# A gated cross-attention and expert block: the routing tiles' copies on ScalarE, their residual on TensorE, a head more on VectorE

## The reference

```python
xn   = layernorm(x)                                   # 4096 tokens x 256
kv   = ctx @ W_kv.T + b_kv                            # per token: 16 keys, 16 values of 16 numbers
s    = einsum('bshd,bstd->bsht', q, k) / 4            # 16 heads attend to 16 heads of the SAME token
co   = einsum('bsht,bstd->bshd', softmax(s), v)
x    = x + tanh(g_xattn) * (co @ W_out.T + b_out)
xn   = layernorm(x)
p    = softmax(xn @ gate_w.T)                         # 8 experts; each takes its 64 best of 256 tokens
h    = gelu(xn[chosen] @ w1[e]) @ w2[e]               # 256 -> 1024 -> 256
x    = x + tanh(g_ffn) * scatter_add(p[chosen] * h)
```

## Time and profile before

| | |
|---|---|
| time, median of 3 runs | 699.21 us (699.01 to 699.41) |
| profiled execution, its own time | 700.73 us |
| span of its trace | 698.7 us |
| mean granted PE clock | 0.976 of full speed |
| busy: PE, DVE, ACT, POOL | 660.8, 597.7, 433.0, 535.4 us |

### The profile page before, as it was taken

One profiled execution on the slowest core, in us unless ns is written; L12 is line 12 of the kernel. 1 busy time (PEld: TensorE's weight loads), 2 busy tenths in 40 slices (PEclk: granted clock), 3 DMA queues, 4 the chain that ended last, 5 costly groups with the idle time before them and its releaser, 6 DMA issues.

```text
span 698.7 us, 11584 instructions
## 1 busy us (share of the span) xinstructions
PE 660.8 (95%) x3921; PEld 539.8 (77%) x3921; DVE 597.7 (86%) x786; ACT 433.0 (62%) x1081; POOL 535.4 (77%) x498
## 2 busy tenths in 40 slices
PE   8999989978799999989999999989999999999996
PEld 5566566534688888878888888868888899999995
DVE  6999999899999999998999999999999251586763
ACT  5677677655777777766777778747766533232321
POOL 4899899897878888988888889888898516435343
PEclk8999999989999999999999999989999999999999
DMA  3876798461558787776788877767777858999993
GB/s 126 304 260 207 229 306 261 177 242 49 190 181 247 241 268 237 221 229 187 222 245 250 242 242 226 234 173 240 227 233 223 269 177 281 327 311 303 322 269 38
DMA packets 97073, 160.96 MB, mean 230 GB/s; under 512 B 8171, under 2 KB 74486, under 8 KB 97014
## 3 DMA queue, kind: packets, MB, share of 16 engines
q1 hardware_dynamic: 84006, 142.78, 61.1%
q0 software_dynamic: 12288, 16.79, 12.9%
q10 hardware_dynamic: 720, 0.66, 0.3%
HBM read 126.63 MB, written 33.55 MB: 229 GB/s over the span
## 4 chain that ended last, share of the span: by engine, by line
PE 67%; DMA 10%; issue 7%; POOL 6%; DVE 6%; ACT 3%; POOLq 0%; DVEq 0%; ACTq 0%
PE bank L1176 21%; PE bank L1159 19%; DMA out_dram<-ys,ids 8%; PE bank L1086 6%; PE bank L1203 4%; PE bank L1106 4%; PE bank L1039 3%; PE bank L1193 3%; DVE prod_v L492 2%; POOL prod_p L344 2%; PE bank L1145 2%; DVE co L494 1%; PE bank L1118 1%; DMA xg<-xn_scratch,ids 1%; POOL tree_a L352 1%
## 5 line engine op out<-in xcount | busy, mean ns | idle before, releaser
L1159 PE MATMUL bank<-xin,w1in 128*128 128x256 f32 x1536 | 205.0, 291 | 5.3 <-issue 4.9
L1159 PEld LDWEIGHTS bank<-xin,w1in 128*128 128x128 f32 x1536 | 193.8, 196 | 6.8 <-issue 6.1
L1176 PE MATMUL bank<-w2s,hT 128*128 128x256 f32 x768 | 175.4, 382 | 0.0
L415 POOL DMA_INDIRECT out_dram<-ys,ids x64 | 105.0, 1640 | 76.8 <-ACT ys L865 57.7
L1176 PEld LDWEIGHTS bank<-w2s,hT 128*128 128x128 f32 x768 | 142.4, 190 | 17.7
L851 ACT ACTIVATE hT<-bank 128x512 f32<-128x512 f32 x128 | 76.0, 597 | 107.7 <-PE bank L1159 107.1
L494 DVE TENSOR_REDUCE co<-prod_v 128x208 f32<-128x3328 f32 (+2 forms) x32 | 109.7, 3428 | 1.1
L492 DVE TENSOR_TENSOR prod_v<-bank,Ex 128x3328 f32<-128x3328 f32 (+2 forms) x32 | 109.6, 3424 | 0.1
L352 POOL TENSOR_TENSOR tree_a<-prod_p 128x512 f32<-128x512 f32 (+2 forms) x64 | 85.8, 1341 | 4.7
L401 POOL DMA_INDIRECT xg<-xn_scratch,ids x64 | 63.9, 998 | 31.8 <-issue 17.0
L344 POOL TENSOR_TENSOR prod_p<-kvs,q 128x1024 f32<-128x1024 f32 (+2 forms) x28 | 80.1, 2859 | 8.1 <-ACT q L819 6.4
(11 more groups left out here) (157 smaller groups left out, 1150.4 us busy)
## 6 DMA issues: line engine op xcount, KB each, us to landing
w1in<-w_parts SPq DMA_DIRECT2D x128, 512.0 KB, 5.3
w2s<-in_L_ffn_w_dram SPq DMA_DIRECT2D x32, 1024.0 KB, 5.7
w_parts<-w1s SPq DMA_DIRECT2D x32, 512.0 KB, 3.3
w1raw<-in_L_ffn_w_dram SPq DMA_DIRECT2D x32, 256.0 KB, 4.4
out_dram<-x SPq DMA_DIRECT2D x32, 128.0 KB, 4.2
xn_scratch<-xn SPq DMA_DIRECT2D x32, 128.0 KB, 2.5
xt<-in_x_dram SPq DMA_DIRECT2D x31, 128.0 KB, 5.2
ct<-in_ctx_dram SPq DMA_DIRECT2D x28, 128.0 KB, 4.7
```

The lines of the kernel that those rows point to most:

```text
L415: pool.indirect_dma_start(out=out_rows[:, :], out_offset=bass.IndirectOffsetOnAxis(ap=ids[:, g % 2, p * E + e:p * E + e + 1], axis=0), in_ ...
L1159: ins = pe.matmul(HB[k % 2][:, D * f:D * (f + 1)], w1in[:, k, w, c, P * f:P * (f + 1)].bitcast(f32r), xin[:, n % 2, x_, c, :], start=(m == ...
L1176: ins = pe.matmul(dst, hT[:, n % 2, f, cols], w2s[:, n % 2, f, :], start=(f == 0), stop=(f == FC - 1))
```

## The change

For the three tiles before a routing tile (9, 17, 25) `with_x` now holds: PE adds x by the identity product, ACT copies x2 out of PSUM, and DVE's `residual` in tiles 10, 18 and 26 is gone. `take_probs` and the gates of `routes` move from DVE to ACT, as `take_probs` and `take_gates` there, for all four groups. In a routing tile DVE takes 13 heads of the values and POOL three, where it was 12 and four. In the tile behind each (11, 19, 27) DVE takes 13 heads of the scores and POOL three, again for 12 and four. No DMA is added or dropped.

```diff
--- before.py
+++ after.py
@@ -26,7 +26,8 @@
     DC = D // P
     FC = F // P
     PR = BG // 2
-    START, EARLY, LATE, FIRST_ROUTING, ROUTING = (11, 11), (12, 11), (12, 13), (4, 12), (4, 12)
+    NEXT = (13, 13)
+    START, EARLY, LATE, FIRST_ROUTING, ROUTING = (11, 11), (12, 11), (12, 13), (4, 13), (4, 13)
     HR = 8
     HV, HP = max(LATE), H - min(ROUTING)
     EPS = 1e-5
@@ -41,16 +42,16 @@
     R2 = J * R0
     n1 = NT - N0 + 1
     gl = G - 1
-    routing = lambda s: s % TG == 2 and s > TG
     summed = lambda t: 0 < t < N0 - 1
     AHEAD = (14, 16, 23, 30)
     NA = len(AHEAD)
     plain = [u for u in range(NT) if u not in AHEAD]
     order = {u: j for j, u in enumerate(plain)}
-    with_x = lambda t: t < N0 - 2
-    x2_steps = lambda t: 3 * t - min(t, N0 - 2)
+    routing = lambda s: s % TG == 2 and s > TG
+    with_x = lambda t: t < N0 - 2 or routing(t + 1)
+    x2_steps = lambda t: 3 * t - sum(with_x(u) for u in range(t))
     heads = lambda t: (START if t == 0 else FIRST_ROUTING if t == N0 - 1 else EARLY if t < N0 - 1 else
-                       ROUTING if routing(t) else LATE)
+                       ROUTING if routing(t) else NEXT if routing(t - 1) else LATE)
     Sc_count = lambda t: t + 1 + min(t, N0 - 2)
     quarters = lambda s: [divmod(i, Q) for i in range(3 * s + min(s, 2), 3 * s + 3 + min(s + 1, 2))] if s < N0 - 1 else []
     assert 2 * CAP == P and TG == E and BG == 4 and n1 == NE - E - 2
@@ -594,8 +595,6 @@
 
             def take_probs(g):
 
-                dve.wait_ge(prT_psum, g + 1)
-                dve.tensor_copy(work[:, :], XT[0:R2, 0:P]).then_inc(work_ready, 1)
                 wait_apart(work_ready, g + 1)
                 if g > 0:
                     dve.wait_ge(route_psum, g)
@@ -648,10 +647,6 @@
                     rows = slice(CAP * beta, CAP * (beta + 1))
                     dve.tensor_tensor(ids[rows, g % 2, :].rearrange("q (p e) -> q p e", e=E), lists[rows, 0, :, beta, :],
                                       row_base[rows, beta, :].unsqueeze(2).broadcast_to([CAP, PR, E]), ALU.add).then_inc(ids_ready, 1)
-                for beta in range(2):
-                    rows = slice(CAP * beta, CAP * (beta + 1))
-                    dve.tensor_scalar(gts[rows, g % 2, :].rearrange("q (p e) -> q p e", e=E), lists[rows, 1, :, beta, :],
-                                      tanh_g[rows, 1:2], None, ALU.mult).then_inc(gts_ready, 1)
 
             def low_tokens(n):
 
@@ -840,6 +835,22 @@
                 act.wait_ge(gstep, 3 * g + 2)
                 act.activation(pe_[:, :, :, :].rearrange("p j b e -> p (j b e)"),
                                lgs[:, :, :, :].rearrange("p j b e -> p (j b e)"), ACT.Exp).then_inc(gexp_ready, 1)
+
+            def take_probs(g):
+
+                act.wait_ge(prT_psum, g + 1)
+                if g > 0:
+                    act.wait_ge(round_done, CAP // 8 * g)
+                copy(work[:, :], XT[0:R2, 0:P], work_ready)
+
+            def take_gates(g):
+
+                act.wait_ge(ids_ready, 2 * (g + 1))
+                lists = XT[:, T:T + 2 * R0].rearrange("q (v p b e) -> q v p b e", v=2, b=2, e=E)
+                for beta in range(2):
+                    rows = slice(CAP * beta, CAP * (beta + 1))
+                    act.activation(gts[rows, g % 2, :].rearrange("q (p e) -> q p e", e=E), lists[rows, 1, :, beta, :],
+                                   ACT.Copy, scale=tanh_g[rows, 1:2]).then_inc(gts_ready, 1)
 
             def take_xh(n):
 
@@ -934,6 +945,8 @@
                 if routing(s):
                     if n >= 0:
                         take_ctT(s + 1)
+                    take_probs(s // TG - 1)
+                    if n >= 0:
                         gelu(n, 0)
                         gelu(n, 1)
                     take_coT(s - 1)
@@ -951,6 +964,7 @@
                         take_caT(2)
                         take_kva(1)
                     exponentials(s)
+                    take_gates(s // TG - 1)
                     if n >= 0:
                         gelu(n, 2)
                         gelu(n, 3)
@@ -1007,6 +1021,7 @@
             take_logits(NT - 1)
             gate_exp(gl)
             gelu(n, 3)
+            take_probs(gl)
             take_y(n - 1)
             gelu(n + 1, 0)
             gelu(n + 1, 1)
@@ -1016,6 +1031,7 @@
             gelu(n + 1, 3)
             gelu(n + 2, 0)
             gelu(n + 2, 1)
+            take_gates(gl)
             take_y(n + 1)
             take_xh(n + 3)
             gelu(n + 2, 2)
@@ -1099,7 +1115,7 @@
                     pe.wait_ge(bias_moved, 3 * 16)
                 if with_x(t):
                     pe.wait_ge(x_loaded[t % XB], 16 * (t // XB) + 16)
-                    pe.wait_ge(ctT_ready, t + 2)
+                    pe.wait_ge(ctT_ready, order[t] + 2)
                     pe.matmul(S0[:, 0:D], ident[:, :], xt[:, t % XB, :], start=True, stop=False)
                 pe.wait_ge(coT_ready, t + 1)
                 for c in range(DC):
```

## The result

Over 20 runs each, the kernel before had a median of 699.49 us and the changed one 701.81 us. The ratio is 1.0024, with a 95% interval from 1.0015 to 1.0033: 1.7 us slower, between 1.05 and 2.3. It is not the quotient of the two medians, which is 1.0033 (2.3 us). The forecast was 700.3 from a median of 699.21, that is +1.1 us. The profiled execution has a span of 700.7 us, against 698.7 before.

A forecast was written before the change was run, and what follows sets the result against it. In tiles 18 and 26 PE's full queue, then `ids`, then VectorE's products were taken to bound the kernel; 2 x 0.5 + 0.1 = +1.1 us on 699.21 gave 700.3, range 698.4 to 702.0.

The forecast's parts named there:

- PE's product, +0.5 in tiles 18 and 26: PE's identity product, ahead of `route_columns` in a full queue, costs 0.44 to 0.60 us, taken as 0.5 per tile.
- VectorE's relief before `ids` gains nothing: In tiles 18 and 26 VectorE's lists come 0.3 us earlier but only wait longer for PE: gain nothing.
- `ids` to the low parts 8.04, the hole unchanged: VectorE's gates go, a head comes, net 0.0; PE's 2.47 us idle around the gathered rows keeps its length.
- The tile behind: In tile 19 VectorE's 1.64 us wait for POOL before `con` goes; PE does not use it: cost and gain nothing.
- ScalarE: Copy to `work` 0.25 us, gates 0.5 in tile 26; these fit, with half a microsecond to spare before `ys`.
- Tile 10, +0.1; the tail, nothing: Tiles 10 and 11 together +0.1 us (-0.4 to +0.3); in the tail ScalarE's lateness of 0.4 meets 3.7 us spare.
- The rival of the clock: Slow products behind PE's idle time in tile 18 become like tile 26's: +2.0 us in all, 701.2; chance 0.26.
- The expectation of 4.6 and 5.5 us behind the holes: Sign: the first 24 products behind PE's idle times in tiles 18 and 26 still take 4.6 and 5.5 us.

The follow-up runs named there:

- a_again: The changed kernel once more, with no edit, for a second profile; ratio to the kernel before 1.0011.
- a_no_pe: The changed kernel with the residual of tiles 9, 17 and 25 back on VectorE, so without PE's identity product; ratio to the kernel before 0.9997.
- b_dummy: The kernel before with three identity products added on PE ahead of the output projection of tiles 9, 17 and 25; ratio 1.0052.
- a_w1_late: The changed kernel with two late loads of the next expert's first matrix held back until both gathers landed; ratio to the kernel before 1.0003.
- a_route_first: The changed kernel with `route_columns` ahead of `hidden(n, 2)` in PE's list in routing tiles; ratio to the kernel before 0.9964.

## Why the prediction was right, and where its numbers came from

1. **PE's product, +0.5 in tiles 18 and 26.** Right in place and mechanism; the size is 0.43, just below the lower bound of 0.44. `route_columns` of tile 18 was at 306.47, 3.20 later than before, of which 2.77 had come from ahead of tile 18.
2. **VectorE's relief before `ids` gains nothing.** Right: 1.37 and 1.42 us of idle time (forecast 1.2), released by PE. PE came 1.50 and 1.55 us behind the ready lists, for in tile 18 they were ready 0.7 us earlier behind the transposed probabilities and not 0.3 (in tile 26 it was 0.3).
3. **`ids` to the low parts 8.04, the hole unchanged.** VectorE's part is right, gates and head cancel: it was there at 315.27, 8.14 us behind `ids`, and 8.05 with the loads held back (312.58 - 304.53). The two parts alone showed +0.55 and -0.50. But the hole did not stay. The step that fails is the sentence that the hole's length stays because VectorE ends it by 0.2 us; the landing of the gather was taken as fixed, and it came later by more than that margin (0.2 us in tile 18, 0.7 in tile 26). The prediction named it ("one that landed 0.2 us later would cost") and put nothing in the sum. It measured +0.38 and +0.31 us in the two tiles (9.20 and 9.15, against 8.82 and 8.84), 0.7 in all; of each, VectorE's own part is 0.1 and the wait for the gathered rows the rest. In four executions with the lists in their old place and no product ahead of them, the second transpose came 6.30 to 6.75 us behind `ids` in 8 holes of 8; in five with one product or three (the loads not held back) it came at 7.2 to 8.0 in 8 of 10. That what SyncE has in flight delays the gather is shown, the loads being the likely part; why 0.43 us of PE's work moves the gather against them is not.
4. **The tile behind.** Right. `con` of tile 19 at 333.95 has no idle time before it, against 1.64, and PE did not feel it. That row names no releaser (`issue`); that it was POOL's share follows from POOL's own timeline, where the last sum of the values ends at 331.43, 0.09 us before `con`.
5. **ScalarE.** Right: 0.26 us for the copy to `work`, 0.56 for the two gates (forecast 0.5). The time to spare was forecast before `ys`, half a microsecond; it was 0.39 us in both tiles. The 1.36 us idle before `xin` in tile 26 are no margin of ScalarE's, they come of the late gather.
6. **Tile 10, +0.1; the tail, nothing.** +0.1 from 31 us to 188.25, but made of fewer slow products ahead and of 3.06 us of idle time before `hidden` instead of 1.60; that is too mixed to be called confirmed. In a_again the same distance is 0.8 us longer than before (190.06 - 32.56 = 157.50, against 156.69). In the tail VectorE had 3.3 us to spare.

The terms then are 2 x 0.43 + 0.7 + about 0 = 1.6 us, where the times say 1.7 in the first measurement and 0.8 in a_again (1.1 and 1.4 at equal clock), and the forecast 1.1. The forecast's sum thus had one term slightly too large and lacked another. That the measured median, 701.81, lies within the range (698.4 to 702.0) owes something to luck: it is above the forecast's own 699.8 to 700.8, and the room above that had been made for the clock, not for the gather.

The rival of the clock has little to show over many runs: its mean is 0.980 after (0.982 in a_again) and 0.981 before, and 0.001 is 0.3 us. The expectation of 4.6 and 5.5 us behind the holes was wrong as an expectation of one execution. In four executions (before, the change twice, and a_no_pe) the holes were 2.47 to 2.97 us long, and the same 24 products took 3.10, 4.51 to 4.61 or 5.46 us behind them. The Trainium skill says on the page "TensorE: Matmul & The Clock Gate" (Part 1) that the phase is not tied to the kernel. The trace agrees: the same place of the same program took 3.10 and 4.61 us. What was lacking in the prediction is that such a difference belongs in the spread and not among the rivals. It is open why two kernels, the product alone and the heads alone, have means of 0.977 and 0.978: their heads are long, 9.1 to 9.5 us, but one of b_dummy's is longer (9.90, the other 8.83), with a mean of 0.981.

## What to carry over

When two engines both arrive within a few tenths at the point that ends a wait, price the second one too: the change left VectorE's work in that stretch the same length, and the gather, which had been 0.2 and 0.7 us early, took over. Where an engine is full, ask what is queued ahead of the instruction that others wait for; the same product cost 0.43 us a tile ahead of the lists and next to nothing once the lists' product had been moved forward, and the changed kernel with that move is 0.36% faster than the kernel before. Compare timelines between points of the same program and subtract what had come before; one execution's total holds slow products (2.4 us here) that fall elsewhere in the next.

## What the runs showed of the hardware that was not expected

- Two gathers issued 0.64 and 1.97 us behind `ids` had landed 4.75 us behind it where SyncE issued neither load nor store in between (a_w1_late). With two loads of 512 KB issued 0.57 us ahead of `ids` and 1.6 us behind it, and a store of 128 KB behind them, PE's transposes of the second came 6.3 to 8.0 us behind it; with the loads at 1.62 and 3.06 us (a_route_first), at 7.70 and 7.74.
- An identity product of two pieces between other products costs a full queue 0.43 us, 0.215 a piece; the 0.60 to 0.70 us that its row shows are no price, since the rows of neighbouring products overlap.
- After idle times of equal length (2.70 us, twice in one execution) 24 products took 4.60 and 3.12 us.
